# A new order of the work in the cross-attention steps of a transformer block

## The reference

```python
q = _heads(xq @ wq)
k, v = jnp.split(ctx @ wkv, 2, axis=-1)
q, k = _rope(q, sq, cq), _rope(k, sk, ck)
a = jax.nn.softmax(einsum('bhnd,bhmd->bhnm', q, k) * DH ** -0.5, axis=-1)
o = einsum('bhnm,bhmd->bhnd', a, v)          # then heads side by side
return o @ wo + bo
```

## Time and profile before

| | us |
|---|---|
| three runs | 1938.48, 1941.3, 1942.46 |
| median | 1941.3 |
| profiled execution, own time | 1941.05 |
| its span, first to last instruction | 1939.3 |

### The profile page before, as it was taken

One profiled execution on the slowest core, in us unless ns is written; L12 is line 12 of the kernel. 1 busy time (PEld: TensorE's weight loads), 2 busy tenths in 40 slices (PEclk: granted clock), 3 DMA queues, 4 the chain that ended last, 5 costly groups with the idle time before them and its releaser, 6 DMA issues.

```text
span 1939.3 us, 47598 instructions
## 1 busy us (share of the span) xinstructions
PE 1886.7 (97%) x17616; PEld 1319.3 (68%) x17616; DVE 1576.9 (81%) x2316; ACT 965.3 (50%) x1692; POOL 1302.7 (67%) x856
## 2 busy tenths in 40 slices
PE   7999999978999999999999999999999999999999
PEld 4666767756777677777777777767777777777764
DVE  4999999956888888888888888888888888888851
ACT  3455555534545554455555445555554555454444
POOL 4878757415777677777767767767677677766762
PEclk8999999978999999999999999999999999999999
DMA  5322233211111111111111111111111111111110
GB/s 174 118 87 86 86 112 87 73 33 46 53 52 46 46 48 46 53 52 49 52 46 48 46 49 54 49 48 52 46 48 47 52 52 51 52 46 48 45 35 22
DMA packets 141440, 113.28 MB, mean 58 GB/s; under 512 B 62496, under 2 KB 105376, under 8 KB 141216
## 3 DMA queue, kind: packets, MB, share of 16 engines
q1 hardware_dynamic: 104352, 109.95, 16.9%
q10 hardware_dynamic: 36864, 0.28, 1.0%
HBM read 31.21 MB, written 1.05 MB: 17 GB/s over the span
## 4 chain that ended last, share of the span: by engine, by line
PE 84%; DVE 4%; issue 4%; POOL 4%; DMA 2%; ACT 1%; SPq 1%; ACTq 0%; DVEq 0%; POOLq 0%
PE S L1504 24%; PE OB L1518 20%; PE PB L1446 10%; PE PB L1465 9%; PE S L1485 7%; PE PB L1527 2%; PE PB L1432 2%; DMA swapped<-turned 2%; PE PB L1537 1%; PE S L1345 1%; POOL KL L736 1%; PE PB L1311 1%; POOL psum_acc L743 1%; PE OB L1373 1%; PE OB L1356 1%
## 5 line engine op out<-in xcount | busy, mean ns | idle before, releaser
L795 POOL TENSOR_TENSOR psum_acc<-psum_acc,P 124x1024 f32<-124x1024 f32 (+1 forms) x320 | 691.1, 2160 | 179.8 <-ACT P L967 162.4
L967 ACT ACTIVATE P<-S 124x1024 f32<-124x1024 f32 (+1 forms) x448 | 431.3, 963 | 562.5 <-PE S L1504 562.3
L1189 DVE TENSOR_REDUCE mxc<-S 128x2 f32<-128x1024 f32 x384 | 469.6, 1223 | 181.5 <-PE S L1485 181.4
L788 POOL TENSOR_TENSOR psum_acc<-P 124x1024 f32<-124x1024 f32 x64 | 152.6, 2384 | 219.2 <-PE PB L1527 209.4
L1518 PE MATMUL OB<-P,V 124*64 124x256 f32 (+1 forms) x2236 | 289.0, 389 | 0.0
L1504 PE MATMUL S<-QH,KH 64*124 64x256 f32 (+1 forms) x1664 | 273.3, 323 | 6.5 <-ACT P L967 6.0
L1504 PE MATMUL S<-MX,share 64*124 64x256 f32 (+1 forms) x1664 | 238.0, 280 | 0.0
L1504 PE MATMUL S<-QL,KH 64*124 64x256 f32 (+1 forms) x1664 | 237.2, 279 | 0.0
L1504 PE MATMUL S<-QH,KL 64*124 64x256 f32 (+1 forms) x1664 | 237.1, 279 | 0.0
L1504 PEld LDWEIGHTS S<-QH,KH 64*124 64x124 f32 (+1 forms) x1664 | 156.5, 182 | 115.2 <-issue 110.6
L1518 PEld LDWEIGHTS OB<-P,V 124*64 124x64 f32 (+1 forms) x2236 | 145.7, 137 | 93.0 <-issue 28.2
(11 more groups left out here) (176 smaller groups left out, 3514.8 us busy)
## 6 DMA issues: line engine op xcount, KB each, us to landing
swapped<-turned SPq DMA_DIRECT2D x512, 128.0 KB, 2.1
kv_w<-sa_kv_dram SPq DMA_DIRECT2D x64, 128.0 KB, 2.3
qswapped<-qturned SPq DMA_DIRECT2D x128, 64.0 KB, 1.9
ctxT_all<-ctx_dram SPq DMA_DIRECT2D x8, 624.0 KB, 4.7
q_w<-sa_wq_dram SPq DMA_DIRECT2D x64, 64.0 KB, 2.0
q_w<-ca_wq_dram SPq DMA_DIRECT2D x64, 64.0 KB, 2.0
o_room<-ca_wo_dram SPq DMA_DIRECT2D x64, 64.0 KB, 2.0
swapped<-turned SPq DMA_DIRECT2D x128, 16.2 KB, 1.8
```

The source lines that it names most:

```text
L788: pool.tensor_tensor(acc, P_of(J, 0)[0:rows], P_of(J, 1)[0:rows], ALU.add).then_inc(x.acc, 2)
L795: pool.tensor_tensor(acc, acc, P_of(J, c)[0:rows, :, 0:w], ALU.add).then_inc(x.acc, 1)
L967: act.activation(P_of(J, c)[0:rows, :, 0:w], SP[0:rows, :, 0:w], ACT.Exp, scale=SCALE).then_inc(x.e, 1)
L1189: dve.tensor_reduce(mxc[:, t, :, c:c + 1], MP[:, :, 0:w], AX.X, ALU.max).then_inc(x.am, 1)
```

## The change

The five strings of words of CROSS are written anew. On PE, between two groups of scores (`s`, with the `a` beside them) there are now only words of one tile shape: before, `a4 k1 v0 p2 a5` and `a0 v2 n2 s0 a1 k3 v3 p6 s1` had projections and products in one gap. The output projection `o` moves from the step after its exponentials to one later, with its `ad` on DVE (`+-2`). `k0` moves to the end of the iteration for the step after next (`+2`), with `kt0`, `kc0` and the swap. On ACT, `qh` moves behind `e6`, `ve1` and `kh1` stand ahead of `e6`, and `e1`, `e2`, `kh3` are in the iteration of their own scores. On DVE, `ka2`, `kt3`, `kc3`, `kl2` come after `am1`, and `dv` after `am3` and `kl3`. The words of the last step, which are written out, follow suit: the output of step 62 (`b0`) now runs there.

```diff
--- before.py
+++ after.py
@@ -90,14 +90,14 @@
                  "f cp l+3 cc+3 cq cs",
                  "w+4 x+3")
     CROSS = Cross("ca", DC, M, 124, 512,
-                  "a4 k1+1 v0+1 p2+-1 a5 n0 s4+-1 q+1 p3+-1 a6 s5+-1 v1+1 k2+1 p4+-1 n1 p5+-1 s6+-1 a0+1 v2+1 n2 s0 "
-                  "a1+1 k3+1 v3+1 p6+-1 n3 s1 a2+1 k0+2 sum+-1 n4 s2 a3+1 p0 p1 o+-1 s3",
-                  "am4 kc0+1 kt1+1 am5 qt+1 ka0+1 am6 qc+1 kl0+1 nm n0 kc1+1 ka1+1 kt2+1 kc2+1 n1 am0+1 kl1+1 ka2+1 am1+1 "
-                  "kl2+1 kt3+1 am2+1 kc3+1 rc+-1 dv+-1 ka3+1 am3+1 kl3+1 ad+-1 kt0+2",
-                  "wh+3 e1+-1 e2+-1 kh3 e3+-1 ve0+1 e4+-1 kh0+1 e5+-1 mr ve1+1 n0 qh+1 e6+-1 kh1+1 ve2+1 n1 e0 kh2+1 ve3+1 "
-                  "oe+-1 n2 xh",
-                  "c4+-1 qa+1 c5+-1 cf+-1 c6+-1 ql+1 wl+3 c1 xl c2 c3",
-                  "r+4 w+2 k0+1 k1+1 q+1 wo k2+1 k3+1")
+                  "s3+-1 a4 k1+1 v0+1 a5 n0 s4+-1 o+-2 p2+-1 q+1 p3+-1 a6 s5+-1 k2+1 v1+1 n1 s6+-1 a0+1 p4+-1 p5+-1 p6+-1 "
+                  "n2 s0 a1+1 v2+1 k3+1 n3 s1 a2+1 sum+-1 p0 p1 n4 s2 a3+1 k0+2 v3+1",
+                  "am4 ka0+1 kt1+1 kc1+1 am5 ad+-2 kl0+1 qt+1 qc+1 am6 nm ka1+1 n0 kt2+1 kc2+1 am0+1 kl1+1 n1 am1+1 ka2+1 "
+                  "kt3+1 kc3+1 kl2+1 am2+1 ka3+1 rc+-1 am3+1 kl3+1 dv+-1 kt0+2 kc0+2",
+                  "wh+3 e3+-1 ve0+1 kh0+1 e4+-1 e5+-1 mr n0 ve1+1 kh1+1 e6+-1 qh+1 oe+-1 n1 e0 kh2+1 ve2+1 e1 kh3+1 e2 "
+                  "ve3+1 n2 xh",
+                  "c3+-1 c4+-1 qa+1 c5+-1 cf+-1 c6+-1 ql+1 wl+3 c1 xl c2",
+                  "r+4 w+2 k1+1 q+1 wo k2+1 k3+1 k0+2")
     assert B == PAIRS == 2 * UNROLL and LNC == 2 * N and T == GROUP * LNC
     assert all(B * M - b * (M - CW) >= 0 and (M - CW) * b + (512 - 4 * DC) * 3 <= TOK for b in range(B))
 
@@ -999,7 +999,7 @@
                     act.activation(hidden_sb[n % 4], hidden_bank[n % 3][:, :], ACT.Gelu, bias=cols[:, 12 + f:13 + f]
                                    ).then_inc(s_g, 1)
 
-                run_words("e1 e2 e3 out0 e4 out1 e5 out2 e6 g0 g1 oe0 g2 g3 g4 g5 g6 g7 bsquare0 g8 broot0 g9 g10 g11 bout0 "
+                run_words("e3 out0 e4 out1 e5 out2 e6 g0 g1 oe0 g2 g3 g4 g5 g6 g7 bsquare0 g8 broot0 g9 g10 g11 bout0 "
                           "g12 g13 g14 g15", of(do, STEPS - 1), norm(LN3), norm(LNL, "b"), {"g": gelu})
 
             act.wait_ge(s_set, 3)
@@ -1227,8 +1227,9 @@
                     dve.wait_ge(s_f, (c + 1) * FF)
                     add_to_x(xT[:, c * LNC:(c + 1) * LNC], ff_out[c], 10).then_inc(s_y, 1)
 
-                run_words("inverse unit0 unit1 unit2 rc0 dv0 ad0 y0 bcentre0 binverse0 y1 bunit0 y2 y3",
-                          of(do, STEPS - 1), norm(LN3), norm(LNL, "b"), {"y": add_ff})
+                run_words("inverse unit0 unit1 unit2 b0 rc0 dv0 ad0 y0 bcentre0 binverse0 y1 bunit0 y2 y3",
+                          of(do, STEPS - 1), {"b": lambda k: do["ad"](STEPS - 2, k)}, norm(LN3), norm(LNL, "b"),
+                          {"y": add_ff})
 
             do = cross_words()
             dve.wait_ge(s_const, 16 * 5)
@@ -1606,9 +1607,9 @@
                     pe.wait_ge(x.added, STEPS)
                     last["mean"](0)
 
-                run_words("p2 spread0 s4 p3 spread1 s5 p4 spread2 s6 p5 h0 h1 p6 h2 f0 h3 sum0 f1 h4 f2 h5 f3 "
+                run_words("s3 b0 p2 spread0 s4 p3 spread1 s5 p4 spread2 s6 p5 h0 h1 p6 h2 f0 h3 sum0 f1 h4 f2 h5 f3 "
                           "o0 h6 f4 h7 bmean0 f5 h8 f6 bvar0 h9 f7 h10 f8 bspread0 h11 f9 f10 h12 f11 h13 h14 f12 "
-                          "h15 f13 f14 f15", of(do, STEPS - 1), {"spread": chunks_mean["spread"]},
+                          "h15 f13 f14 f15", of(do, STEPS - 1), {"b": lambda k: do["o"](STEPS - 2, k)}, {"spread": chunks_mean["spread"]},
                           {"bmean": last_mean, "bvar": last["var"], "bspread": last["spread"]},
                           {"h": hidden, "f": feed})
```

## The result

| | us |
|---|---|
| before, median of 4 runs | 1940.03 (1938.48 to 1942.46) |
| changed, median of 4 runs | 2227.93 (2224.51 to 2231.39) |
| ratio | 1.148, 95% interval 1.146 to 1.1505 |
| profiled execution of the changed kernel, own time and span | 2231.39 and 2229.6 |

The change costs 288 us. The sign and the waits were forecast (2160), the size was not: the time lies above the range, which ended at 2215.

What follows compares the result with a forecast made beforehand. PE, without slack in the cross stage, was taken as the bound. Over two steps, -1.24 us of switches and the four waits gave +7.1, 3.56 a step, times 62 +221 us: 2160 us. Own range 2085 to 2205, widened to 2000 to 2215.

Steps and rivals of the forecast that it cites:

- e6: Not a run: the exponentials on ACT that need scores s6; forecast to start at s6+1.20 us, ahead of qh.
- switches of shape: PE's tile shape switches fall from 18 to 14 a step, which saves 0.62 us a step.
- a0 on QH, with refilling: Every step, PE waits at a0 for QH, copied behind the exponentials e6: stall 1.6 us, 1.7 with refilling the array.
- q on ad, with a5: q waits for DVE's ad: stall 0.5 us after an even pair, 2.0 with refilling after an odd one.
- v3 on dv: In even pairs only, v3 waits for the division dv on DVE: stall 1.06 us, with refilling 1.15.
- sum on ve2: Every step, sum waits for V's read ve2, behind kh2 on ACT: stall 0.6 and 0.7 us.
- e before s1 and s3: Exponentials e1 to e5 were said to be covered by other PE matmuls; e0 of odd pairs misses by 0.07 us.
- What bounds the kernel: In the cross stage PE has no slack, so every microsecond its order costs or waits is one of the end.
- The four waits: PE stalls at a0 on QH, v3 on dv, q on ad and sum on ve2: 3.4, 1.15, 2.5, 1.3 us per two steps.
- the rival of the clock: Idle gaps on PE make its clock fall: 4 us a fall, one for two steps +130 us, 2290; chance 4%.
- keep their cover: Words other than a0, v3, q and sum stay covered; e0 of odd pairs misses by 0.07 us.

Runs made afterwards that it cites:

- the three DVE edits: Changed kernel with, one at a time on DVE, dv ahead of am3 (2225.31 us), ka2 ahead of am1 (2213.18 us), ad right behind am5 (2168.72 us).
- the run without waits: The run with mr ahead of qh, with p4 ahead of s6 on PE and further moves on ACT, DVE and POOL: 1912.74 us.
- The filler: Changed kernel with 12 additional matmuls that nobody reads, where a0 waits for QH on PE: 2174.34 us.

## Why the prediction was right and wrong

Per step, forecast and measured in the changed kernel (distances of starts, less those where nothing waits):

| | forecast | measured |
|---|---|---|
| switches of shape | -0.62 | about -0.68, as the remainder |
| a0 on QH, with refilling | 1.70 | 1.73 (2.19 for 0.57, and 0.11) |
| q on ad, with a5 | 1.25 | 1.47 (2.13 for 0.87, v0 to a5 1.01 for 0.80) |
| v3 on dv | 0.58 | 0.58 (k to v 1.03 for 0.80, 150 times in 60 steps) |
| sum on ve2 | 0.65 | 0.70 |
| e before s1 and s3 | 0.04 | about 0.24 |
| clock | 0 | 0.57 (p4 to s0 2.88 for 2.31), and 0.05 (a0 to p4 0.50 for 0.44) |
| all | 3.6 | 4.66 (27.39 for 22.73) |

*What bounds the kernel* held: PE has no slack, and each wait put on it showed whole. *The four waits* held, in place, engine and size; three are within 0.05 us a step. One word moved in the kernel before (qh behind e6) and one moved back in the changed one (qh first) bear out the first from both sides, the three DVE edits the others. *The switches*: the run without waits shows a gain, 0.43 us a step with 15 switches. That it is 0.6 with 14 isn't measured, since no run with 14 was free of waits. It rests on the remainder above, and on the run with mr ahead of qh: its step of 22.60, less the 0.45 that a0 lost, would be 22.15, 0.58 under the kernel before.

*The step that failed* is the rival of the clock, "The clock falls ... Against: the new gaps leave PE busy over 80% of a step, not 54%. 4%." I put it as another outcome beside the waits, with one reason against it that looks at a whole step. It wasn't a rival but a term of the sum: the clock fell 24 times in 60 steps, 23 of them at the end of a0's gap. Fall for fall it was cheaper than I said (1.6 us, not 4). Without it, 0.62 us a step are off, and 38 of the 66 us by which 2162 missed 2228. The comparison was also with too few rows. The stretch of the ramp that I quoted had 3.0 us idle in 6.5, and the gap ahead of a0 has 1.45. That showed that so much idle time can come before a fall, not that less would be harmless.

The other 28 us are small terms: q's wait (0.22 a step), and the exponentials before s1 and s3, which I had said to "keep their cover" (0.2). I had worked out q's wait with the median landing of k's swaps, 2.1 us. Where they land so, p2 to q takes 1.4 or 2.5 us in turn; where they land later, up to 4.0 us after the issue, it takes up to 3.4, and nothing makes up for that: the shortest of the 60 is 1.37. The range's own upper end, 2205, had only longer waits in it, and 2215 not the clock.

The Trainium skill ("TensorE: Matmul & The Clock Gate", section "Why this matters for your kernels") tells to avoid idle gaps of PE between bursts of matmuls, since the clock then falls back. The trace agrees with its direction. It warns only of longer gaps than these, however, and there the measurement decides: the clock fell behind gaps of 1.45 us idle, and in one run of 1.1.

What stays open: why the clock falls at one a0 and not at the next with the same gap of 1.45 us. Taking out another wait raised the count (33 with dv early, 37 with ka2 early), taking out q's lowered it (18). The falls often come in rows, one in two steps (at 528.2, 582.8, 637.4, 692.1, 746.7 and 801.3 us), so it may hang on where the gap lies in time; no run tested that. What the runs do tell is that gaps are the cause. Over the same 60 steps, the changed kernel and the six runs that each change only one or two things in it have 117 falls between them. 108 begin within 0.1 us before to 1.2 after the start of a0, behind 1.45 to 1.8 us idle, and nine within 0.3 us before to 0.8 after the start of q, behind 1.8 to 2.2 us idle. None begins elsewhere.

## What to carry to other kernels

Where TensorE is never idle, an order that saves switches between tile shapes is worth what the distances of starts say (0.14 to 0.20 us each; three of them gave 0.43 us a step), but only after each word's last supplier has been followed through the in-order queues of the other engines: one copy behind one exponential cost 104 us, all else equal. Move the other engines' words with PE's, and give a copy that hangs on a DMA more room than the median landing. A gap that comes back in every step, like these of 1.1 and 1.45 us, can have a second price, the clock, and can hide what another repair is worth; a few matmuls that nobody reads, put into the gap, measure it.

## What the runs showed of the hardware that was not expected

- More matmuls made the kernel faster: twelve in each a0 gap, 54 us less.
- The clock fell at the end of gaps of 1.45 us idle in 23 of 60 steps, and some 1.5 us after the end of gaps of 1.1 us in 8 of 60. A fall cost 1.6 us in the changed kernel and 2.5 to 3 in the kernel before with qh late.
- After a wait within one shape, some 0.1 us more are lost: from a0 to the next word it takes 0.44 us, and 0.33 where a0 didn't wait (in the kernel before, and in the run with p4 ahead of s6). The filler doesn't take this away (0.44).
